# First attention: VectorE copies the value sums out of PSUM instead of ScalarE, ahead of the fourth row maximum of a round, and VectorE's rounds are written out without a loop

## The reference, cut to what matters

```
qkv  = jnp.einsum('bld,ed->ble', x, w_qkv) + b_qkv          # x: layer-normalised, 2 x 2048 x 256
q, k, v = split into 16 heads of 16 features
attn = softmax(jnp.einsum('blhc,bmhc->bhlm', q, k) * SCALE)  # 2 x 16 x 2048 x 2048, float32
heads = jnp.einsum('bhlm,bmhc->blhc', attn, v)               # the value sums
```

## Time and profile before

| | us |
|---|---|
| median of 3 runs | 2477.73 (2476.5 to 2492.4) |
| the profiled execution, its own time | 2464.94 |
| its span in the profile | 2463.2 |
| the 32 rounds of the first attention, about | 1364 of the span |
| TensorE / VectorE / ScalarE busy, whole span | 90% / 75% / 59% |

### The profile page before, as it was taken

One profiled execution on the slowest core, in us unless ns is written; L12 is line 12 of the kernel. 1 busy time (PEld: TensorE's weight loads), 2 busy tenths in 40 slices (PEclk: granted clock), 3 DMA queues, 4 the chain that ended last, 5 costly groups with the idle time before them and its releaser, 6 DMA issues. The chain is left out here.

```text
span 2463.2 us, 44369 instructions
## 1 busy us (share of the span) xinstructions
PE 2211.5 (90%) x14912; PEld 1233.5 (50%) x14912; DVE 1840.1 (75%) x3240; ACT 1448.6 (59%) x2165; POOL 463.5 (19%) x673
## 2 busy tenths in 40 slices
PE   7786799999999999999999999988999986799988
PEld 5564333333333333333333333326888875566688
DVE  5553999999999999999999999913443565788846
ACT  4443177777777777777777777771222222266743
POOL 0000000000000000000000000003455510266745
PEclk8998599999999999999999999999999988589999
DMA  6766700310500500402205002006567469666564
GB/s 212 260 238 196 93 4 6 47 22 5 61 5 8 61 3 12 57 6 36 31 5 61 7 8 61 3 5 188 155 172 177 103 235 355 130 134 154 153 166 129
DMA packets 189121, 231.80 MB, mean 94 GB/s; under 512 B 72720, under 2 KB 122768, under 8 KB 186064
## 3 DMA queue, kind: packets, MB, share of 16 engines
q1 hardware_dynamic: 176048, 210.46, 35.0%
q10 hardware_dynamic: 7184, 14.10, 2.8%
q0 software_dynamic: 5728, 5.00, 0.9%
HBM read 138.97 MB, written 89.13 MB: 93 GB/s over the span
## 5 line engine op out<-in xcount | busy, mean ns | idle before, releaser
L1015 DVE TENSOR_REDUCE a_maxes<-a_ps_a 128x2 f32<-128x1024 f32 x1024 | 1202.3, 1221 | 112.0 <-PE a_ps_a L1136 108.3
L1080 ACT ACTIVATE a_prob<-a_ps_s 128x512 f32<-128x512 f32 (+1 forms) x1376 | 1035.8, 804 | 347.5 <-PE a_ps_s L1162 341.5
L1162 PE MATMUL a_ps_s<-a_Q,a_K 50*128 50x512 f32 x2048 | 593.8, 452 | 90.7 <-ACT a_prob L1080 90.4
L1136 PE MATMUL a_ps_a<-a_K,a_Q 48*128 48x512 f32 x2048 | 549.9, 454 | 25.6 <-DMA a_Q<-s_halves 14.2
L1174 PE MATMUL a_ps_o<-a_prob,a_V 128*17 128x512 f32 x4096 | 539.8, 599 | 0.1
L1162 PEld LDWEIGHTS a_ps_s<-a_Q,a_K 50*128 50x128 f32 x2048 | 277.4, 185 | 505.8 <-ACT a_prob L1080 456.6
L1136 PEld LDWEIGHTS a_ps_a<-a_K,a_Q 48*128 48x128 f32 x2048 | 244.9, 189 | 229.7 <-issue 107.9
L973 POOL DMA_DIRECT2D a_Q<-a_m_parts x128 | 64.5, 504 | 1285.3 <-DVE a_m_parts L1007 1278.6
L1626 ACT ACTIVATE a_prob<-a_ps_s 128x512 f32<-128x512 f32 (+1 forms) x256 | 135.7, 583 | 111.6 <-PE a_ps_s L1717 110.5
L1566 DVE CUSTOM_DVE_ANT_0 a_scratch<-a_ps_a,k_mask 128x256 f32<-128x256 f32 (+1 forms) x512 | 177.9, 411 | 30.0 <-PE a_ps_a L1681 28.0
L1681 PE MATMUL a_ps_a<-k_K,k_Q 48*128 48x256 f32 (+1 forms) x512 | 122.2, 363 | 32.5 <-PEq L89 21.7
(11 more groups left out here) (186 smaller groups left out, 2225.3 us busy)
## 6 DMA issues: line engine op xcount, KB each, us to landing
s_halves<-p_parts SPq DMA_DIRECT2D x64, 512.0 KB, 5.3
s_xT<-p_xT SPq DMA_DIRECT2D x64, 256.0 KB, 4.4
a_Q<-s_halves SPq DMA_DIRECT2D x186, 64.0 KB, 10.4
a_K<-s_halves SPq DMA_DIRECT2D x42, 256.0 KB, 9.6
s_v<-p_v_out SPq DMA_DIRECT2D x16, 544.0 KB, 4.5
s_cT<-p_cT SPq DMA_DIRECT2D x32, 256.0 KB, 3.6
k_wb<-s_w SPq DMA_DIRECT2D x16, 512.0 KB, 7.6
c_wb<-s_w SPq DMA_DIRECT2D x16, 512.0 KB, 7.2
```

What stands on the lines that cost most here:

```text
L1015: nc.vector.tensor_reduce(maxes[:, :, slot, qt, kc], ps_a[:, o:o + 2 * CH].rearrange("p (z k) -> p z k", z=2), AX.X, ALU.max).then_inc(a_d ...
L1080: nc.scalar.activation(prob[:, ring:ring + len(t), :].rearrange("p r q -> p (r q)"), ps_s[:, bank:bank + len(t) * CH], ACT.Exp, scale=scal ...
L1136: last = nc.tensor.matmul(ps_a[:, o + side * CH:o + (side + 1) * CH], Q[rows, q0:q0 + P], K[rows, k0:k0 + CH], start=True, stop=True)
L1162: last = nc.tensor.matmul(ps_s[:, bank + x * CH:bank + (x + 1) * CH], K[rows, k0:k0 + P], Q[rows, q0:q0 + CH], start=True, stop=True)
```

## The change

VectorE gets `copy_output`, as a `tensor_copy` with the same two waits, at position 3 (`COPY_AT` is now a position, 3) ahead of the maximum of that position; in round r it copies the sums of round r - 1, from round 1 on. ScalarE's copies go, from its loop and from behind it. VectorE's `Fori` over 15 pairs of rounds becomes a Python loop over 30 rounds, so that its program is written out and its waits are on constants. The last two copies stand ahead of the last two `normalise`. Nothing else is touched; TensorE's, GpSimd's and SyncE's instructions stand in the same order as before.

```diff
-    UNIT_LAG, LAG, LATE, COPY_AT = 1, 24, 1, 2
+    UNIT_LAG, LAG, LATE, COPY_AT = 1, 24, 1, 3
...
         @block.vector
...
+            def copy_output(it):
+                dve.wait_ge(pv_done, KT * (it + 2))
+                dve.wait_ge(o_turned, it + 1)
+                nc.vector.tensor_copy(oT[:], ps_o[:]).then_inc(oT_ready, 1)
+
             def iteration(it, parity, more):
                 for p in range(NPOS):
+                    if p == COPY_AT and it > 0:
+                        copy_output(it - 1)
...
-            with dve.Fori(0, NIT // 2 - 1) as i:
-                iteration(2 * i, 0, True)
-                iteration(2 * i + 1, 1, True)
+            for it in range(NIT - 2):
+                iteration(it, it % 2, True)
             iteration(NIT - 2, 0, False)
+            copy_output(NIT - 2)
             normalise(NIT - 1, bank_of(0, 1))
+            copy_output(NIT - 1)
             normalise(NIT, bank_of(0, 0))
...
         @block.scalar
...
-            def copy_output(it):
-                act.wait_ge(pv_done, KT * (it + 2))
-                act.wait_ge(o_turned, it + 1)
-                nc.scalar.activation(oT[:], ps_o[:], ACT.Copy).then_inc(oT_ready, 1)
...
                         exponential(2 * i + r, r % 2, j)
-                        if j == COPY_AT:
-                            copy_output(2 * i + r - 1)
             for j in range(NJ):
                 exponential(NIT - 1, 1, j)
-                if j == COPY_AT:
-                    copy_output(NIT - 2)
-            copy_output(NIT - 1)
```

## The result

The changed kernel takes 2515.8 us (median of 4 runs, 2506.0 to 2527.1), before 2479.4 (4 runs, 2476.5 to 2492.4). The ratio is 1.0158, with a 95% interval of 1.0126 to 1.0191: slower, by 1.6%. The profiled execution took 2506.0 us, 41.1 more than the one of before.

A forecast was written before the change was run, and what follows sets the result against it. TensorE was taken as fullest (40.00 of 42.70 us a round), with VectorE in step; 30 delays of 1.28 us at the in-order first value step add 38.4 to the 2477.7 median: 2516 us, range 2496 to about 2530.

The forecast's parts named there:

- The forecast step: Whole-kernel slowdown: 30 copies, in rounds 1 to 30, each delay TensorE by 1.28 us, +38.4 us.
- ScalarE's relief: Removing the 0.60 us copy from ScalarE each round: it lay in a gap, so worth 0.
- Start and length of the copy: VectorE's copy stands behind the maximum of position 2, starts 1.13 us after that maximum's start and lasts 0.68 us.
- the two-input row: Profile row of a 128x512 VectorE operation with one PSUM and one SBUF input, 0.683 us, used for the copy's length.
- The stall: Start of each round: first value step loads 1.28 us later, TensorE's queue behind it shifts too, nothing comes back.
- The gap ahead of the maximum of position 4: VectorE stands idle there for 0.6 us each round, because unit 4 comes 1.28 us later.
- The loop: VectorE's loop instructions, 0.18 us a pass, 15 times, are hidden, so writing the rounds out is worth 0.
- The end of the phase: Round 31 has no maxima: first value step at about 1625.14 instead of 1625.08; with the final copy, together 0.
- VectorE's spare time: Rival: VectorE's idle 3.8 us a round takes the copy in, giving 2494 us, or 2478 if all comes back; chance 0.14.
- ScalarE did not hold the rounds: Denies the rival that ScalarE held the rounds, whose relief would take off 18 us, giving 2460 us; chance 0.05.
- The dearer copy: Rival: copy or its start costs more, or the clock falls; over 1.65 us a round, 2528 us and up; chance 0.07.

The follow-up runs named there:

- ScalarE behind exponential 4: Kernel before the change, with ScalarE's copy moved two exponentials later, from behind exponential 2 to behind exponential 4; 2540.7 us (1 run).
- a copy and a half: Changed kernel, with VectorE first copying 256 columns and then, after a wait on that, all 512; 2595.1 us (1 run).
- the copy twice: Changed kernel, with VectorE doing the full copy two times, the second waiting for the first; 2584.7 us (1 run).
- the late one: Changed kernel, with VectorE's copy one position later, ahead of the maximum of position 4; 2611.8 us (1 run).

## Why the prediction was right, point by point

- **The time.** 2516 was forecast, 2515.8 measured. Part of that closeness is luck: the four runs spread over 21 us, and the base was a median of three; beside the changed kernel the one of before had 2479.4, so by the medians the step is 36.4. The forecast step, 38.4 us, is confirmed without that scatter, by 38.3 us between the first and the last `whole_maxima`.
- **ScalarE's relief is worth 0.** Right. The exponential behind the old copy kept its distance to its scores, and the kernel without any copy has the same round.
- **Start and length of the copy.** Start forecast 1.13 us behind the start of the maximum of position 2, measured 1.14 (875.53 to 876.67). Length taken as 0.68 from the two-input row, measured 0.681. By the table in the Trainium skill ("VectorE: DVE Perf Modes", section "The TRN2 errata — SBUF-src ops pay a fixed extra latency per instruction") the estimate was 0.658, 0.02 too little; half the copy at 0.415 fits one element per cycle at 0.96 GHz, which the same table has, with a fixed part of 0.148 us where the table has 0.125.
- **The stall.** 1.28 us forecast, 1.28 measured, and nothing came back: the second value step stands 2.59 us behind the first. The gap ahead of the maximum of position 4 was put at 0.6, it is 0.68.
- **The loop.** Worth 0, as forecast: 42.69 us a round with the written-out program alone. The 15 branches for which the Trainium skill ("Advanced Engine Details and Errata", section "Control Flow Timing") gives an estimate of 1.6 us earn nothing here: they lie beside the maxima.
- **The end of the phase.** In round 31 the first value step comes 1.87 us behind the last instead of 1.77, 0.10 more where 0.06 was forecast; nothing on this scale.
- **The rivals.** VectorE's spare time takes nothing in: the slope in the copy's length is near one, from half a copy to two, at full clock. ScalarE did not hold the rounds. The dearer copy did not come, and the clock stayed at 1.00 in every round of the changed kernel. But I dismissed the clock for a poor reason: I argued from the busy share over 54 us, and the experiments show the clock fall shortly behind a short stall, in rounds in which TensorE has the same 40 us of work. The changed kernel has a stall of 1.2 us and keeps its clock in this trace; the kernels with 1.6 and 1.7 don't. The chance of 0.07 covered that; the argument did not.

## What to carry to other kernels

When a small operation moves to another engine, its price is not its length against that engine's spare time but when it is done against when the in-order queue that needs it arrives there: find the last moment at which it costs nothing (here, by the rows, about 0.3 us after the old copy's end: the first value step could load at 900.09, 0.40 us behind that end, and needs 0.06 from the copy) and count what stands ahead of it in its new queue. One position earlier the same copy on the same engine cost 0.08 us a round instead of 1.27. And a wait that the trace puts down to an instruction is only its doing if the time fits: leave the instruction out, and see whether the wait goes.

## What the runs showed of the hardware that had not been expected

TensorE's clock gave way to a stall much shorter than I had looked for. With the rest of the round unchanged (TensorE busy for 40 of about 44 us), with a stall of 1.2 us (time without a matmul; the loads sat idle for 1.65) the clock stayed at 2.4 GHz in all 30 rounds. With 1.6 us it fell to 1.2 GHz in 3 of 30 (ScalarE behind exponential 4), with 1.7 in 21 of 30 (a copy and a half), with 1.9 in 23 (the copy twice), and with 2.4 in all 30 (ahead of position 4). These are counts from one execution of each kernel, and they are not rates: with ScalarE behind exponential 4, stalls of 1.62 to 1.68 us passed without a fall in 27 rounds, and the three falls came behind stalls of 1.62, 1.62 and 1.67 us. So something beside the stall's length decides, and that 1.7 us is worse than 1.6 is not shown. A round in which it fell was mostly 1.2 to 3.4 us longer, up to twice the 1.7 us of the delay itself. The Trainium skill, "TensorE: Matmul & The Clock Gate", section "HAM oscillation — how this bites in real kernels", also has idle gaps bring the clock down for the work behind them, and the direction agrees; the gaps in its example are longer than these; here stalls of 1.6 to 2.4 us had a fall behind them, in part of the rounds or in all.

The twice-copied kernel and the late one took 69 and 96 us more than the changed kernel for 0.7 and 1.1 us more of delay a round. A copy and a half, with 0.45 us more of delay a round, took 79 us more, 2.6 us a round: where the clock falls as well, a change of half a microsecond in one wait can cost several times its own size.
